# Transposing the normalised rows y by 32x32 blocks on VectorE, by way of DRAM, instead of on TensorE

## What is computed

```python
def layernorm(x): m, v = mean(x), var(x); return (x - m) / sqrt(v + 1e-5)   # over the last axis

def attention(text, features, Wq, bq, Wk, bk):
    Q = text @ Wq.T + bq; K = features @ Wk.T + bk
    attn = softmax(Q @ K.T / sqrt(1024))
    return attn @ features

def ffn(y, qweight, qzeros, scales, bias, g_idx):
    w = nibbles(qweight);  zeros = nibbles(qzeros) + 1
    weights = scales[g_idx] * (where(w > 0, 1., -1.) - zeros[g_idx])        # 1024 x 1024
    return y @ weights + bias

x = x + attention(layernorm(x), ctx, ...)     # called x1 in the kernel
x = x + ffn(layernorm(x), ...)                # layernorm(x) is called y
```

## Time and profile before

| | |
|---|---|
| median of 3 runs | 574.36 us (573.82 to 575.12) |
| the profiled execution, its own time | 574.79 us |
| span of the profiled execution, first to last instruction | 573.0 us |
| mean granted TensorE clock | 0.999 of full speed (2.4 GHz) |
| TensorE busy | 564.5 us, 99% of the span |
| VectorE, ScalarE, GpSimd busy | 389.3, 217.5 and 187.5 us (68%, 38%, 33%) |

### The profile page before, as it was taken

The page is one execution under the profiler, slowest core; times in us unless marked ns, Lnnn a source line. Parts: engine busy times, 40 slices in busy tenths (PEclk is TensorE's granted clock), DMA queues, the critical chain, the costliest instruction groups (busy, mean ns, idle before and its releaser), DMA issues.

```text
span 573.0 us, 7564 instructions
## 1 busy us (share of the span) xinstructions
PE 564.5 (99%) x2798; PEld 466.2 (81%) x2798; DVE 389.3 (68%) x627; ACT 217.5 (38%) x410; POOL 187.5 (33%) x135
## 2 busy tenths in 40 slices
PE   7999999999999999999999999999999999999997
PEld 6888888787777877778898999987878888888886
DVE  4977775789889997855225444776987668668342
ACT  6964444310531512433347666644222122212210
POOL 2071000000000000000336777777844742752630
PEclk9999999999999999999999999999999999999999
DMA  8851100459587535834444899997011430310111
GB/s 283 245 165 57 37 1 0 148 149 291 183 269 233 193 152 186 254 111 186 145 186 162 307 363 349 329 398 294 2 73 74 146 108 41 148 73 13 61 74 73
DMA packets 39027, 94.01 MB, mean 164 GB/s; under 512 B 3096, under 2 KB 17440, under 8 KB 36816
## 3 DMA queue, kind: packets, MB, share of 16 engines
q1 hardware_dynamic: 32464, 87.25, 41.7%
q10 hardware_dynamic: 6528, 6.29, 5.0%
HBM read 59.98 MB, written 33.55 MB: 163 GB/s over the span
## 4 chain that ended last, share of the span: by engine, by line
PE 91%; DVE 4%; issue 1%; ACT 1%; DMA 1%; SPq 0%; ACTq 0%; DVEq 0%
PE bank L1164 23%; PE bank L1166 23%; PE bank L1165 23%; PE bank L1208 5%; PE bank L1214 5%; PE bank L1211 5%; PE bank L1266 2%; PE bank L1332 2%; DMA wk_stage<-in_L_xattn_Wk 1%; DVE stats L842 1%; DVE xres L1035 1%; PE bank L1249 1%; DVE yin L1072 1%; PE bank L1174 1%; PE bank L1250 1%
## 5 line engine op out<-in xcount | busy, mean ns | idle before, releaser
L1164 PE MATMUL bank<-xT_hi,m_hi 128*128 128x512 f32 x256 | 104.4, 408 | 0.0
L1166 PE MATMUL bank<-xT_hi,m_lo 128*128 128x512 f32 x256 | 101.0, 395 | 0.0
L1165 PE MATMUL bank<-xT_lo,m_hi 128*128 128x512 f32 x256 | 100.7, 394 | 0.0
L1118 DVE TENSOR_TENSOR xres<-xres,bank 128x512 f32<-128x512 f32 x56 | 38.5, 687 | 45.8 <-PE bank L1166 45.7
L521 POOL TENSOR_TENSOR l_lo_s<-l_sum_s,l_hi_s 128x512 fp32r<-128x512 f32 x32 | 42.4, 1356 | 71.1 <-DVE l_sum_s L1054 71.1
L490 POOL TENSOR_TENSOR pairs<-mv,pairs 128x2 f32<-128x2 f32 x16 | 11.1, 695 | 164.0 <-DVE mv L847 163.5
L705 ACT ACTIVATE t_pair<-bank,ucol 128x512 f32<-128x512 f32 x32 | 22.0, 688 | 111.7 <-PE bank L1166 106.4
L507 POOL TENSOR_TENSOR tT_lo<-t_pair,tT_hi 128x1024 fp32r<-128x1024 f32 x16 | 39.1, 2461 | 76.7 <-ACT tT_hi L546 76.7
L1164 PEld LDWEIGHTS bank<-xT_hi,m_hi 128*128 128x128 f32 x256 | 48.1, 188 | 12.7 <-issue 0.2
L1166 PEld LDWEIGHTS bank<-xT_hi,m_lo 128*128 128x128 f32 x256 | 48.1, 188 | 11.3
L1165 PEld LDWEIGHTS bank<-xT_lo,m_hi 128*128 128x128 f32 x256 | 48.1, 188 | 11.2 <-issue 0.2
(11 more groups left out here) (144 smaller groups left out, 1266.7 us busy)
## 6 DMA issues: line engine op xcount, KB each, us to landing
cin<-in_ctx SPq DMA_DIRECT2D x8, 1024.0 KB, 5.5
xres<-in_x SPq DMA_DIRECT2D x8, 1024.0 KB, 11.2
out<-xres SPq DMA_DIRECT2D x15, 512.0 KB, 2.7
right_scratch<-part_hi SPq DMA_DIRECT2D x28, 256.0 KB, 2.2
xn_scratch<-xin SPq DMA_DIRECT2D x6, 1024.0 KB, 5.0
xq<-xn_scratch ACTq DMA_DIRECT2D x24, 256.0 KB, 5.4
r_tile<-right_scratch SPq DMA_DIRECT2D x6, 1024.0 KB, 11.0
xin<-in_x SPq DMA_DIRECT2D x5, 1024.0 KB, 7.2
```

Source lines behind the costliest of these rows:

```text
L1118: dve.tensor_tensor(part, part, prod_bank(f, n)[:, :], ALU.add).then_inc(s_acc, 1)
L1164: pe.matmul(out_, a_hi, b_hi, start=start, stop=False, skip_group_check=True)
L1165: pe.matmul(out_, a_hi, b_lo, start=False, stop=False, skip_group_check=True)
L1166: return pe.matmul(out_, a_lo, b_hi, start=False, stop=stop, skip_group_check=True)
```

## The change

In the first stage the rows of x already go through DRAM to be transposed on VectorE (`load_quadrants`, `x_blocks`, L873). The change does the same for y of the batches 2 to 7. The batches 0 and 1 stay on TensorE.

- TensorE: `y_tr` is called only for batches 0 and 1. Six groups of sixteen transposes go away.
- ScalarE: `y_apply` moves here for all eight batches, as an activation y = rstd * x1 + shift, where shift = -mean * rstd. For f >= 2 it writes its columns in another order. It comes ahead of `a21_copy` of the batch before it, in the two first cases at places of their own.
- VectorE: `y_stats` gets one more small `tensor_scalar` (nmean = -mean). `y_blocks(f + 1, name)` makes four `transpose` instructions, 128x512 each, from the tile `yq` into PSUM banks 4 to 7: two between `y_stats(f + 2)` and `added(f, 2)`, two between `added(f, 2)` and `added(f, 3)`. The sixteen `y_apply` are gone.
- GpSimd: after the power, a small multiplication makes `shift`. The power now stands between the two `add_bias` of a batch instead of behind both.
- SyncE's queue: at the head of turn f, for g = f + 2: store `yin` (1 MB) to DRAM, wait until it landed, and load it back in four pieces of 256 KB with each 32-column quadrant on its own 32 partitions. These stand ahead of the stores of the output of turn f.

```diff
@@ sync
             for f in range(B):
+                g = f + 2
+                if g < B:
+                    sp.wait_ge(s_yn, QT * (g + 1))
+                    sp.dma_start(yn_dram[g].rearrange("(t p) f -> p t f", p=P), yin).then_inc(s_ynst, 16)
+                    sp.wait_ge(s_ynst, 16 * (g - 1))
...
+                    rows = yn_dram[g].rearrange("(m j) f -> j m f", j=32)
+                    for a in range(4):
+                        sp.dma_start(yq[g % 2][32 * a:32 * a + 32, :, :], rows[:, :, a * S:(a + 1) * S]
+                                     ).then_inc(s_yql[g % 2], 16)
                 for t, n in enumerate((5, 6)):
@@ gpsimd
+                    pool.tensor_tensor(rstd, mv[:, :, 1], power, ALU.pow).then_inc(s_rpow, 1)
+                    pool.wait_ge(s_rpow, n - B + 1)
+                    pool.tensor_tensor(shift, nmean, rstd, ALU.mult).then_inc(s_rstd, 1)
...
-                    add_bias(f + 1)
+                    add_bias(f + 1, 0)
                     if f + 2 < B:
                         rsqrt(B + f + 2)
+                    add_bias(f + 1, 1)
@@ scalar
+            def y_apply(f, t):
+                act.wait_ge(s_rstd, B + f + 1)
...
+                else:
+                    act.wait_ge(s_ynst, 16 * (f - 2))
...
+                act.activation(out_, in_, ACT.Identity, bias=shift[:, t:t + 1], scale=rstd[:, t:t + 1]).then_inc(s_yn, 1)
...
             for b in range(1, B):
+                if b > 1 and b + 1 < B:
+                    y_apply(b + 1, 1)
+                    y_apply(b + 1, 0)
                 a21_copy(b)
                 for name in L_HI:
+                    if b == 1 and name == "s3":
+                        y_apply(2, 1)
+                        y_apply(2, 0)
                     left_hi(b, name)
@@ vector
+                if negated:
+                    dve.tensor_scalar(nmean, mv[:, :, 0], -1.0, None, ALU.mult)
...
+            def y_blocks(f, name):
+                t, d = int(name[1]) - 1, int(name[2]) - 1
+                if name == "a21":
+                    dve.wait_ge(s_yql[f % 2], 64 * (f // 2))
+                    dve.wait_ge(s_lhi, N_PROD * f)
+                cols = slice(d * HALF // 4, (d + 1) * HALF // 4)
+                dve.transpose(y_bank(f, name)[:, :].rearrange("p (k m j) -> p m k j", k=4, m=4),
+                              yq[f % 2][:, 4 * t:4 * t + 4, cols].rearrange("p m (k i) -> p m k i", k=4)).then_inc(s_yb, 1)
...
                 if f + 2 < B:
                     y_stats(f + 2)
+                if 0 < f < B - 1:
+                    y_blocks(f + 1, "a21")
+                    y_blocks(f + 1, "a22")
                 if f > 0:
                     added(f, 2)
+                if 0 < f < B - 1:
+                    y_blocks(f + 1, "a11")
+                    y_blocks(f + 1, "a12")
                 added(f, 3)
...
-                if f + 2 < B:
-                    y_apply(f + 2, 1)
-                    y_apply(f + 2, 0)
                 added(f, 5)
@@ tensor
-                    if b + 1 < B:
-                        if n == 3:
-                            y_tr(b + 1, ("a21", "a22", "a11", "a12"))
+                    if b == 0 and n == 3:
+                        y_tr(1, ("a21", "a22", "a11", "a12"))
```

More of the change, by code:

```diff
@@ L94, in xattn_ffn_kernel @@
         jcol = at("jcol", 1.09375, [P, NB], F32)
+        nmean = at("nmean", 1.125, [P, QT], F32)
+        shift = at("shift", 1.15625, [P, QT], F32)
         m_hi = at("m_hi", 2, [P, NB, D], F32R)
@@ L180, in xattn_ffn_kernel @@
         yin = at("yin", 58, [P, QT, D], F32)
+        yq = [at(f"yq{i}", kb, [P, NB, S], F32) for i, kb in enumerate((182.25, 190.25))]
         bias_rows = at("bias_rows", 200.25, [P, D], F32)
@@ L222, in xattn_ffn_kernel @@
         s_yn, s_bias = sem("yn_done"), sem("bias_loaded")
+        s_rpow, s_ynst = sem("ln_rstd_of_y"), sem("yn_stored")
+        s_yql = [sem(f"yn_reloaded{i}") for i in range(2)]
+        s_yb = sem("yn_transposed_by_blocks")
         s_ytr, s_a21, s_lsum = sem("yn_transposed"), sem("a21_copied"), sem("left_sums")
@@ L526, in add_bias @@
                 pool.wait_ge(s_yn, QT * (f + 1))
-                for t in range(QT):
-                    pool.tensor_tensor(x1_of(f)[:, t, :], x1_of(f)[:, t, :], bias_rows, ALU.add).then_inc(s_rb, 1)
-            add_bias(0)
+                pool.tensor_tensor(x1_of(f)[:, t, :], x1_of(f)[:, t, :], bias_rows, ALU.add).then_inc(s_rb, 1)
+            add_bias(0, 0)
+            add_bias(0, 1)
             ctx_lo(B - 1)
@@ L743, in left_hi @@
                 else:
-                    act.wait_ge(s_ytr, 4 * b + 1 + ("a21", "a22", "a11", "a12").index(name))
+                    y_made(act, b, ("a21", "a22", "a11", "a12").index(name))
                     copy(l_hi[name], y_bank(b, name)[:, :]).then_inc(s_lhi, 1)
@@ L758, in _ @@
                     t_hi(b + 1, 1)
+                    if b == B - 2:
+                        y_apply(0, 1)
+                        y_apply(0, 0)
                     c_hi(b + 1, 2)
@@ L771, in _ @@
             left_hi(0, "s4")
+            y_apply(1, 1)
+            y_apply(1, 0)
             act.wait_ge(s_pv, 4 * B)
@@ L1063, in y_stats @@
                     dve.wait_ge(s_x1l[f - KH], 16)
[L1064 to L1074 removed]
+                wait(dve, s_yn, QT * f)
+                ln_stats(x1_of(f), True)
+            def y_blocks(f, name):
[6 more added lines that the diff above has]
+                              yq[f % 2][:, 4 * t:4 * t + 4, cols].rearrange("p m (k i) -> p m k i", k=4)).then_inc(s_yb, 1)
             for b in range(B):
@@ L1085, in _ @@
                         invert_sum(0)
-                    if b == B - 2:
-                        y_apply(0, 1)
                     c_lo(b + 1, 2)
@@ L1098, in _ @@
                     residual(b - 1, 1)
-                    if b == B - 2:
-                        y_apply(0, 0)
                     residual(b - 1, 2)
@@ L1128, in _ @@
                     residual(B - 1, 1)
-                    y_apply(1, 1)
                     residual(B - 1, 2)
                     residual(B - 1, 3)
-                    y_apply(1, 0)
                     left_lo(f, "a22")
```

49 lines of the change are left out of this document (30 added, 19 removed).

## The result

| | before | changed |
|---|---|---|
| median | 574.38 us (4 runs, 573.82 to 575.12) | 580.39 us (4 runs, 580.13 to 580.76) |
| ratio, 95% interval | | 1.0104 (1.0087 to 1.0122) |
| span of the profiled execution | 573.0 us | 578.8 us |

The change made the kernel 6 us slower, where 564.9 was forecast with a range up to 570.9. The forecast of the span was 563.6, so for the profiled span of 578.8 us there are 15.2 us to be found.

A forecast was written before the change was run, and what follows sets the result against it. TensorE's own work was taken as the bound in the turns. The span was 573.0 - 10.5 - 0.53 + 1.4 + 0.2 = 563.6 us; 1.79 above it and 0.43 less for the median gave 564.9, range 562.5 to 570.9.

The forecast's parts named there:

- The work moved to ScalarE: Third-stage turns: two y_apply of 1.06 us each on ScalarE stay hidden, product 6's addition ending 0.6 us early.
- ScalarE is late: Rival, chance 0.07: strided reading above 1.33 us each delays a21 and added(f, 4), 0.3 to 0.8 us in five turns.
- The rival of the slower reload: Chance 0.05: y returns from DRAM too late, VectorE waits, each us is paid six times; 579.9 us at an 18.5 us trip.
- The transposes that go: Turns 1 to 6: each group of transposes taken off TensorE saves 1.75 us, 10.5 us in all.
- The wait in turn 0: Turn 0, product 5: TensorE's 0.53 us loss to a late VectorE addition is regained.
- The small instructions: VectorE, each turn: L847 and nmean take 0.1 us each, neither held up by GpSimd.
- Transposes of 0.60 from start to start: VectorE in the turns: each new 128x512 block transpose to PSUM takes 0.60 us, bounds 0.53 and 1.2.
- Rival two: VectorE becomes the bound within a turn, chance 0.17: transposes take 1.2 us, giving 570.9 us, up to 572.5.
- 0.28 us a turn at product 4: Turns 1 to 5: product 4 waits for added(f, 2) behind two transposes, costing 0.28 us each, 1.4 us in all.
- The way through DRAM: Storing and reloading y ends 4 us before need, about 1 us for batch 2; nothing counted.
- End of the second stage: TensorE's 0.95 us wait for residual(5, 0) stays, with two y_apply ahead of ScalarE's copies; 0.2 us more counted.
- The sum: Whole kernel: all terms give a span of 563.6 us, and 564.9 us against the median of the runs.

The follow-up runs named there:

- the run without a step: The changed kernel with y_apply reading and writing without a stride, leaving y's columns in another order (another output): 564.66 us, ratio 0.9822.
- all of the step moved to the transposes: The changed kernel with plain y_apply; VectorE's block transposes and TensorE's transposes of y read every 8th element instead: 569.87 us, ratio 0.9920.
- `y_apply` put later: The changed kernel with y_apply of batches 3 to 7 later in ScalarE's order, ahead of the copy for s3 instead of a21_copy: 589.97 us, ratio 1.0270.
- the step on the writing side: The changed kernel with y_apply's loops exchanged, so it reads without a stride and writes with one; same result: 574.82 us, ratio 0.9997.
- batch 0 back on VectorE: The changed kernel with both y_apply of batch 0 as tensor_scalar on VectorE, all others still on ScalarE: 576.49 us, ratio 1.0020.

## Why the prediction was wrong

**The step that failed** is the first one of "The work moved to ScalarE": *two `y_apply` of 1.06 each (L546 copies of 128x1024 take 1053 ns)*, with an upper bound of 1.33 from what "the same reading" cost VectorE. It measured 2.42. Neither row covered the case. The copies of L546 read without a step. L1072 did read every 8th element, at 1327 ns, but it is another engine and another instruction. It was read as if the step cost little, and a line of the same trace says otherwise: L868, VectorE's normalisation of the rows of x, is the same `tensor_scalar` with the same two operations, reads in one piece and writes in runs of 32.

```profile
L868 DVE TENSOR_SCALAR xin<-xraw,mv,pairs x6: 807/808/814, 117.4 to 215.3; 128x1024 f32<-128x1024 f32 x6
```

So the step took VectorE from 0.81 to 1.33 us, 1.64 times as long. By the same factor the copy of 1.06 would come to 1.74 on ScalarE (an estimate from these rows): still below 2.42, but 1.4 us more for the pair, where the spare was 0.6. Whether VectorE's `tensor_scalar` follows the rule of 16 bytes is not shown; no distance between was run.

Against a spare of 0.6, both 1.06 and 1.33 were too low, by 2.7 and 2.2 us a pair. The spare of 0.6 us per turn was put in words ("at 1.33 each the spare is 0.1"), so the edge was known and only the price was wrong. 2 x (2.42 - 1.06) = 2.7 us less 0.6 gives 2.1 us a turn; measured are 1.73 us of excess gap at product 6.

The rival "ScalarE is late" named the mechanism and got 0.07 and "0.3 to 0.8" a turn, since its price was bounded by the same row. The rival of the slower reload did come in part, for batch 2: its spare, about 1 us in the prediction and 1.4 in the run without a step, was spent by `y_apply` being slow, its own pair and that of batch 1. Both are one cause, and the prediction treated them as independent.

There was a rule for it, which the prediction didn't weigh. The Trainium skill (SBUF — State Buffer, Door 1: The DMA port swizzle; and Advanced Engine Details and Errata, Memory Cachelines) says that SBUF has lines of 16 bytes, and that an access stream needs two hits on a line for full bandwidth. Runs here agree on ScalarE: at every 2nd float32 1.32 us, at every 4th 2.23, at two out of eight 1.35, against 1.24 plain. The passage of the SBUF page also says that one can stride over 4 float32 for free; the 2.23 us at every 4th contradict that, and the measurement decides.

**The steps that held**, each by its row:

- *The transposes that go*, 1.75 us a group: with no step a turn was 19.57 us, forecast 19.6.
- *The wait in turn 0*: gone, 0.53 us regained.
- *The small instructions* at 0.17 and 0.16, the second in turn 2 starting 0.08 after the first.
- *Transposes of 0.60 from start to start*: 1.22 for two (460.31 to 461.53). Rival two, 1.2 us each, would have come with a step in their read, as "all of the step moved to the transposes" showed; for what the change wrote it didn't come.
- *0.28 us a turn at product 4*: 0.22 measured in turns 2 to 5.
- *The way through DRAM*: a store landed in 4.0 us by the median, a load in 4.7; in turns 2 to 6 VectorE had no wait for it, and with `y_apply` put later the wait came.
- *End of the second stage*: the mechanism was right (two `y_apply` ahead of c_hi), the size went with the failed term. With no step the wait is 0.9, as before.
- *The multiplication on GpSimd* was taken as 0.70 like the power. It is 0.19; this only gave time.
- *The sum*: 564.66 measured without the step, 564.9 forecast. That it is so close is in part luck: `y_apply` was 1.24 there and not 1.06, which the spare hid, and the second stage and product 4 came out a little better than forecast.

One more size was missing from the sum, and belongs to no term: in two places a long wait was followed by slower matmuls, 3.2 of the 15.2 us (last section).

## What to carry to other kernels

When work moves to another engine, price it by a row of that engine *with that access pattern*; where no such row exists, look in the trace for the same instruction with and without the pattern, even on another engine, and carry over at least the ratio, not the absolute time of that engine; the spare has to stand against that. Count the elements that an access takes from each 16 bytes of SBUF: with fewer than two, a float32 instruction of ScalarE or a transpose of VectorE took 1.6 to 2.0 times as long here, and a reordering can often be split between producer and consumer so that neither pays. An idle share says little about an engine that gets its work late: ScalarE was busy 44% of the span and still set the turn, since 4.7 us of it came in one piece ahead of a 0.6 us copy for which everything waited.

## What the runs showed of the hardware

Durations are those of one instruction; in a pair the second starts before the first ends, so half of a pair's time is up to 0.06 less.

- ScalarE, float32, 128x1024 in SBUF, scale and bias by pointer: 1.24 us plain; 1.32 at every 2nd element, read or written; 2.23 at every 4th; 2.42 at every 8th; 2.18 at every 16th; 1.35 to 1.43 in runs of two out of eight. It costs on the writing side too: 2.27 where the step stood there (32 or 128 elements apart).
- VectorE's 32x32 transpose from SBUF to PSUM, float32, 128x512: 0.69 us plain or at every 2nd element, 1.09 at every 4th, 1.21 at every 8th. 128x1024 over two banks: 1.24. Writing PSUM in pieces of 32 elements cost next to nothing: 0.61 from start to start, against a quarter of the 2310 ns of L873 in the earlier trace rows.
- VectorE's `tensor_scalar`, float32, 128x1024 in SBUF: 0.81 us without a step (L868), 1.33 reading every 8th element (L1072).
- TensorE's transposes reading every 8th float32: 275 ns against 272.
- After a wait TensorE's pace can drop. After the 2.76 us of turn 1 the matmuls from 441.79 to 444.78 stood 0.43 apart instead of 0.23, and the windows show the granted clock (the figure ahead of the last two):

```profile
440.00:445.00 5.00, 3.90 (x10) 3.08 (x11) 4.72 (x8) 4.17 (x6) 0.00 (x0) 0.66 0.56 158
445.00:450.00 5.00, 5.00 (x23) 4.08 (x23) 3.17 (x5) 1.31 (x4) 0.09 (x1) 1.00 0.85 301
```

From 441.80 to 444.70 alone the granted clock is 0.50. So at the 2.4 GHz level a start follows the last by 0.23; 0.43 is the 1.2 GHz level, held for about 3 us here, and 1.7 us on top of the wait. The same came after the 3.17 us of the second stage (0.50 from 383.70 to 386.70), the 2.70 us that the step on the writing side left there, the 2.71 us of turn 1 with batch 0 back on VectorE, and the waits of 2.5 to 2.8 us in the run with `y_apply` put later. After the waits of 1.6 us in turns 2 to 5, and the 1.86 us mentioned, it did not.

It does not seem to come in every execution of one kernel, and that would explain the wide spreads above. With batch 0 back on VectorE, three of the ten executions had a mean granted clock of 0.999 to 1.000 and took 574.2 to 574.7 us; the other seven had 0.996 or 0.997 and took 576.3 to 577.2. With the step on the writing side two of ten had 1.000 (572.9 and 573.5 us), the others 0.994 to 0.997 (574.1 to 576.5). Only one execution of each has a trace, so that the lower clock stood behind the same wait in the others is inferred.
